# Graph network on one core: zero fills move from the counting loop to the front and to ScalarE, four table words are read at once, two large copies are issued in parts

## The reference

```python
x = x + attention_over_edges(layernorm(x), edge_weight1, src, dst, ...)  # 8 heads, softmax per destination, then an FFN
x = x + moe(layernorm(x), top 2 of 8 experts, D=256)
x = x + gnn(layernorm(x), edge_index, ...)    # two layers: h = (x + segment_sum(x[src], dst) / deg) @ W.T + b
x = x + moe_ln(layernorm(x), top 2 of 8 experts, hidden 1024)
```

## Time and profile before

| | us |
|---|---|
| median of 3 runs | 2374.04 (2373.87 to 2379.93) |
| the profiled execution | 2378.78 |
| its span | 2377.0 |
| TensorE busy over the span | 2022.4 (85%) |
| `front`, start to last VectorE instruction | 0 to 98.1 |
| `adjacency`, first to last TensorE instruction | 100.0 to 395.1 |
| fills, SyncE's 20 issues | 120.5 to 335.0 |
| the three large copies, issued | 335.5 to 339.4 |

### The profile page before, as it was taken

One profiled execution on the slowest core, in us unless ns is written; L12 is line 12 of the kernel. 1 busy time (PEld: TensorE's weight loads), 2 busy tenths in 40 slices (PEclk: granted clock), 3 DMA queues, 4 the chain that ended last, 5 costly groups with the idle time before them and its releaser, 6 DMA issues. The chain is left out here.

```text
span 2377.0 us, 46115 instructions
## 1 busy us (share of the span) xinstructions
PE 2022.4 (85%) x10757; PEld 1611.7 (68%) x10758; DVE 1399.4 (59%) x3191; ACT 1199.6 (50%) x2508; POOL 848.9 (36%) x859
## 2 busy tenths in 40 slices
PE   7777865888888888869996495799999889999995
PEld 4444433666666666548885385799899877888885
DVE  8688876899999999883445435457425364111111
ACT  2488865777777777622323343455455433222221
POOL 3200000777777777511000667350131303031233
PEclk9899998999999999989995698899999989999998
DMA  4234451777777777510000675434334445565664
GB/s 158 82 151 169 167 191 71 204 206 207 206 208 208 206 206 207 158 47 1 3 1 1 228 219 170 120 107 124 100 104 121 154 158 184 196 219 200 218 225 150
DMA packets 154791, 359.75 MB, mean 151 GB/s; under 512 B 23634, under 2 KB 107415, under 8 KB 150615
## 3 DMA queue, kind: packets, MB, share of 16 engines
q1 hardware_dynamic: 98664, 202.78, 25.6%
q0 software_dynamic: 45520, 145.80, 21.7%
q10 hardware_dynamic: 10528, 10.23, 1.3%
HBM read 276.75 MB, written 78.00 MB: 149 GB/s over the span
## 5 line engine op out<-in xcount | busy, mean ns | idle before, releaser
L1024 POOL DMA_INDIRECT kv_pair<-kv,gather_idx x448 | 440.7, 984 | 147.7 <-issue 131.0
L3401 PE MATMUL ge_p<-ge_y_high,ge_counts_wide 128*128 128x256 f32 (+1 forms) x1250 | 325.1, 298 | 3.7 <-ACT ge_counts_wide L2692 1.7
L1133 PE MATMUL p_edge_q<-QX_kept,onehot_turned 128*128 x904 | 263.0, 414 | 72.1 <-ACT onehot_turned L1096 68.4
L3401 PE MATMUL ge_p<-ge_y_low,ge_counts_wide 128*128 128x256 f32 (+1 forms) x1250 | 309.3, 286 | 0.0
L1133 PEld LDWEIGHTS p_edge_q<-QX_kept,onehot_turned 128*128 128x128 f32 x904 | 154.6, 191 | 178.1 <-issue 163.0
L3401 PEld LDWEIGHTS ge_p<-ge_y_high,ge_counts_wide 128*128 128x128 f32 x1250 | 243.1, 194 | 7.8 <-DVE R_kept L2897 2.4
L3401 PEld LDWEIGHTS ge_p<-ge_y_low,ge_counts_wide 128*128 128x128 f32 x1250 | 243.6, 195 | 1.3
L1141 PE MATMUL p_sums<-R_kept 128*128 128x265 f32 x896 | 237.6, 387 | 0.3 <-DVE R_kept L1034 0.3
L901 PE MATMUL adj_p<-adj_onehot_src,adj_onehot_key 128*128 128x416 f16 x1030 | 204.1, 345 | 30.7 <-issue 15.7
L3527 PE MATMUL ge_p<-ge_y,ge_pack 128*128 128x256 f32 x928 | 213.0, 389 | 8.3 <-ACT ge_column_sums L2790 4.6
L2692 ACT CAST ge_counts_wide<-ge_counts 128x1664 fp32r<-128x1664 uint16 (+1 forms) x100 | 152.6, 1527 | 125.5 <-PE ge_p L3401 125.5
(11 more groups left out here) (615 smaller groups left out, 3791.7 us busy)
## 6 DMA issues: line engine op xcount, KB each, us to landing
ge_pack<-experts SPq DMA_DIRECT2D x29, 2052.0 KB, 8.7
ge_counts<-adj SPq DMA_DIRECT2D x400, 104.0 KB, 2.3
adj<-adj_counts SPq DMA_DIRECT2D x100, 208.0 KB, 1.9
slots_in<-R_kept SPq DMA_DIRECT2D x10, 896.0 KB, 3.6
slots_out<-R_kept SPq DMA_DIRECT2D x10, 896.0 KB, 3.6
experts_rows<-slots_in SPq DMA_DIRECT2D x30, 256.0 KB
ge_column_sums<-slots_in SPq DMA_DIRECT2D x30, 256.0 KB, 6.7
slots_out<-experts_y ACTq DMA_DIRECT2D x29, 256.0 KB, 2.6
```

Of the source, the lines that this page charges most:

```text
L1024: pool.indirect_dma_start(kv[r][:, j, :], None, a["kv"], bass.IndirectOffsetOnAxis(ap=idx[r][:, j:j + 1], axis=0)).then_inc(kv_in[r], 16)
L1133: mm = pe.matmul(pQ[q][:, j, 0:QW], oht[q][:, j, :], QX[:, at(w), :].squeeze(1), start=True, stop=True)
L3401: mm = pe.matmul(bank[:, off:off + D], wide[parity][:, j * P:(j + 1) * P], part[:, at(m), :].squeeze(1), start=opening and off == 0 and pa ...
```

## The change

1. **Fills.** The 20 fills of `slots_in` and `slots_out` leave SyncE's loop. ScalarE issues them in `front`, one ahead of each of the tiles 2 to 21, before that tile's copy of the next `hT`. It waits once that `R` is zero, and at the end of the block for all 20 to have landed.
2. **Words.** Each of the three engines reads four packed words with one load at the head of a turn, in place of one word per window. ScalarE is one window ahead, so its group starts at window 1 of the turn; its last, unrolled turn loads three.
3. **Sums and row numbers.** The zeros for `ACC` go in ten parts of two rows of 26 (271 KB each), one behind each of the turns 0 to 9, and one part of six rows behind turn 9. `WHERE` goes the same way behind the turns 10 to 19 (131 KB each) and a last part of six rows.

```diff
+        zeros_set, slots_filled = sem("zeros_set"), sem("slots_filled")
+        FILL_FROM, FILLS = 2, 10
+        slots = [a[name].rearrange("(p r) d -> p r d", p=P) for name in ("slots_in", "slots_out")]
+        PART = slots[0].shape[1] // FILLS
...
-            pool.memset(k["R"][:], 0.0)
+            pool.memset(k["R"][:], 0.0).then_inc(zeros_set, 1)
...
             act.wait_ge(units_set, HR)
+            act.wait_ge(zeros_set, 1)
             for n in range(NT):
                 b = n % 2
+                if 0 <= n - FILL_FROM < 2 * FILLS:
+                    table_, part = divmod(n - FILL_FROM, FILLS)
+                    act.dma_start(slots[table_][:, at(PART * part, PART), :],
+                                  k["R"][:, 0:PART, :]).then_inc(slots_filled, 16)
                 if n + 1 < NT:
                     copy_turned(n + 1)
...
+            act.wait_ge(slots_filled, 16 * 2 * FILLS)
...
-            packed = eng.value_load(k["WTAB"][0:1, at(w)], min_val=0, max_val=128 * VPACK - 1)
+        def words_of(kind, w, count):
+            return nc.values_load_multi_w_load_instructions(k["WTAB"][0:1, at(w, count)], engines=[kind], min_val=0,
+                                                            max_val=128 * VPACK - 1)[1]
...
+        def over_windows(eng, kind, step_of):
+            with eng.Fori(0, TURNS) as i:
+                words = words_of(kind, TURN * i, TURN)
+                for b in range(TURN):
+                    step_of(words[b], TURN * i + b, b, i)
...
-            for s_ in range(2):
-                with sp.Fori(FILLS * s_, FILLS * (s_ + 1)) as i:
-                    for b in range(TURN):
-                        window(TURN * i + b, b, i)
-                    sp.dma_start(slots[s_][:, at(PART * i - PART * FILLS * s_, PART), :],
-                                 k["R"][:, 0:PART, :]).then_inc(zeros_out, 16)
...
-            sp.dma_start(sums[:, over:], zeros).then_inc(zeros_out, 16)
-            sp.dma_start(sums[:, 0:over], zeros[:, 0:over]).then_inc(zeros_out, 16)
-            sp.dma_start(k["WHERE"][:].rearrange("p n c -> p (n c)"), a["places"]).then_inc(zeros_out, 16)
+            with sp.Fori(0, FILLS) as i:
+                for b in range(TURN):
+                    window(TURN * i + b, b, i)
+                zero_sums(at(SPREAD * i, SPREAD), SPREAD)
+            zero_sums(slice(DONE, NT + 1), NT + 1 - DONE)
+            with sp.Fori(FILLS, 2 * FILLS) as i:
+                for b in range(TURN):
+                    window(TURN * i + b, b, i)
+                sp.dma_start(k["WHERE"][:, at(SPREAD * i - DONE, SPREAD), :],
+                             places[:, at(SPREAD * i - DONE, SPREAD), :]).then_inc(zeros_out, 16)
+            sp.dma_start(k["WHERE"][:, DONE:, :], places[:, DONE:, :]).then_inc(zeros_out, 16)
...
-            last_onehot(0, 0, 0)
-            with act.Fori(0, NW // TURN - 1) as i:
+            last_onehot(words_of(ENG.Activation, 0, 1)[0], 0, 0)
+            with act.Fori(0, TURNS - 1) as i:
+                words = words_of(ENG.Activation, TURN * i + 1, TURN)
```

More of the change, by code:

```diff
@@ L764, in adjacency @@
     nc, a, C = k["nc"], k["a"], k["C"]
-    TURN = 4
+    TURN, ENG = 4, mybir.EngineType
     with ExitStack() as s:
@@ L816, in window, with zero_sums @@
                 sp.dma_start(a["adj"][at(w)].rearrange("o q d s -> (o q d) s"), out[b][:]).then_inc(stored[b], 16)
-            for s_ in range(2):
-                with sp.Fori(FILLS * s_, FILLS * (s_ + 1)) as i:
-                    for b in range(TURN):
-                        window(TURN * i + b, b, i)
-                    sp.dma_start(slots[s_][:, at(PART * i - PART * FILLS * s_, PART), :],
-                                 k["R"][:, 0:PART, :]).then_inc(zeros_out, 16)
-            zeros, sums = (t[:].rearrange("p n c -> p (n c)") for t in (k["R"], k["ACC"]))
-            over = sums.shape[1] - zeros.shape[1]
-            sp.dma_start(sums[:, over:], zeros).then_inc(zeros_out, 16)
-            sp.dma_start(sums[:, 0:over], zeros[:, 0:over]).then_inc(zeros_out, 16)
-            sp.dma_start(k["WHERE"][:].rearrange("p n c -> p (n c)"), a["places"]).then_inc(zeros_out, 16)
+            def zero_sums(rows, count):
+                sp.dma_start(k["ACC"][:, rows, :].rearrange("p n c -> p (n c)"),
+                             zeros[:, 0:count * VWC]).then_inc(zeros_out, 16)
+            zeros = k["R"][:].rearrange("p n d -> p (n d)")
+            SPREAD = (NT + 1) // FILLS
+            DONE = SPREAD * FILLS
+            with sp.Fori(0, FILLS) as i:
[9 more added lines that the diff above has]
+            sp.dma_start(k["WHERE"][:, DONE:, :], places[:, DONE:, :]).then_inc(zeros_out, 16)
             with sp.Fori(2 * FILLS, TURNS) as i:
@@ L842, in _, with window @@
             low = C[:, C_IOTA:C_IOTA + P].unsqueeze(1).to_broadcast(wide)
-            def window(w, b, i):
+            def window(word, w, b, i):
                 p = b % 2
-                f, m, v0 = chunks_of(dve, w, TURN // 2 * i + b // 2)
+                f, m, v0 = chunks_of(word, TURN // 2 * i + b // 2)
                 with dve.Fori(0, m) as j:
@@ L858, in window @@
                         ins.then_inc(last_made[p], 1)
-            over_windows(dve, window)
+            over_windows(dve, ENG.DVE, window)
             dve.wait_ge(root_ready, 1)
@@ L882, in _, with window @@
         def _(pe):
-            def window(w, b, i):
+            def window(word, w, b, i):
                 p = b % 2
-                _, m, v0 = chunks_of(pe, w, TURN // 2 * i + b // 2)
+                _, m, v0 = chunks_of(word, TURN // 2 * i + b // 2)
                 def add_nothing(first):
@@ L904, in window @@
                 add_nothing(False).then_inc(summed, 1)
-            over_windows(pe, window)
+            over_windows(pe, ENG.PE, window)
         @block.scalar
```

27 lines of the change are left out of this document (12 added, 15 removed).

## The result

The changed kernel took 2364.23 us (median of 6 runs, 2361.44 to 2365.69); the kernel before, on the same chip, 2376.07 us (6 runs, 2372.23 to 2380.06). The ratio is 0.9948, with an interval of 0.9934 to 0.9962: faster by 0.5%, about 12 us, and half of the 23.7 us forecast. The measured 2364.23 lies 0.2 us above the range given. The profiled execution took 2365.69 us, its span is 2363.9.

A forecast was written before the change was run, and what follows sets the result against it. TensorE bounds front; in adjacency engines wait for each other, with gaps from register loads during fills. Gains 14.7 + 11.0, less 1.0 for parts and 1.0 for front, make 23.7 us: forecast 2350.3 us, range 2342 to 2364.

The forecast's parts named there:

- The bound: In adjacency no engine is full; engines wait for each other through buffer pairs, and register loads slow down during fills.
- Fills and large copies: Counting turns in adjacency: moving fills and splitting large copies gains 14.7 us, 6.2 from fills and 8.5 from copies.
- if every turn takes the 10.36 us of the quiet two: Adjacency: all 24 turns were given the mean of two late turns without fills, 10.63 and 10.08 us, totalling 248.6 us.
- Words: Adjacency: reading four words per load shortens turns from 10.36 to 9.90 us, gaining 11.0 us; other end 19.7.
- if it costs as one, it is in the 9.90: Loop head in adjacency: a four-word load priced like a single load adds nothing beyond the 9.90 us turn.
- the rival of words priced as whole loads: Loop head: each word costs a full load, from no change (2372) to slower (2392); chance 0.04, mild form 0.04.
- the way from 10.36 us down to VectorE's own work: Adjacency turns: removing three of four loads per engine can gain towards VectorE's 9.42 us, plus the changes of window.
- my own term of 0.46 us a turn: Adjacency: gain per turn from bunched words, 10.36 to 9.90 us, with 0.12 us gaps at four windows; 24 turns, 11.0 us.
- Small parts: Zeros and row numbers spread behind 20 adjacency turns cost 1.0 us, between 0 and 1.8 us.
- Front: Twenty fills issued by ScalarE in front cost 1 us, between 0 and 8; DMA share 0.97, issues fit in 1.40 us.
- rival about the DMA engines: In front, DMA at 300 rather than 404 GB/s lands the last fill late, costing 8 us, 2357; chance 0.08.
- the issue: Rival in front: ScalarE held at each issue until its fill lands, 44 us lost against 24.7 gained, 2393; chance 0.02.

The follow-up runs named there:

- e1: Changed kernel with packed words read one by one again, fills in front and small parts kept: 2349.01 us, ratio 0.9910 to the kernel before.
- e3: Kernel before with only the zeros of the sums and the row numbers in small parts; fills stay in the loop: ratio 0.9960.
- e4: Kernel before with only the 20 fills moved to ScalarE in the front; large copies and single words kept: ratio 0.9946.
- e7: Changed kernel with two words per load on all three engines, two loads a turn: median turn 10.38 us, ratio 0.9935 to the kernel before.
- e9: Changed kernel with ScalarE checking its four words' bounds twice, eight more register instructions at the loop's head: median turn 11.54 us, 2383.07 us in one run.
- after: The changed kernel itself, in its first measurement and profile: 2364.23 us, ratio 0.9948 to the kernel before, median turn 10.67 us.
- e8: The changed kernel unchanged, measured again on another chip: ratio 0.9941 to the kernel before, median turn 10.67 us.
- e10: Changed kernel with ScalarE reading its four words by four single loads at the loop's head: median turn 11.25 us, 2380.83 us in one run.
- e5: Changed kernel with four words at once on ScalarE only, one per window on VectorE and TensorE: median turn 11.23 us, ratio 1.0025 to the kernel before.

## Why the prediction was wrong

**The bound.** Right in kind: in `adjacency` the engines wait for each other, and the gaps with no releaser come with loads and grow with fills. e1 and e3 show it directly, 9.2 us of such gaps on ScalarE without fills, 17.7 with them.

**Fills and large copies: the mechanism right, the term too small.** The sum gave 14.7 us less 1.0 for the parts; e1 shows 21.6. The step that failed is "if every turn takes the 10.36 us of the quiet two". The two were 10.63 and 10.08 us, the first of them the turn right behind the stall. Without fills turns take 9.96 us (e4) or 9.97 (e1). So the fills were worth some 0.70 us a turn, not 0.31: over the first 20 turns e4 takes 13.7 us less than before (212.87 and 226.54), where the sum had 6.2. For the large copies the sum had 8.5, and e3, parts included, shows 9.2: 10.0 less over the last four turns, 0.8 more over the first 20.

**Words: the wrong sign.** The sum gave a gain of 11.0 us; it was a loss of 14.8. Two steps failed. The first is "if it costs as one, it is in the 9.90". It doesn't: the head went to 1.82 us, past the 1 us at which the text said the forecast would be wrong, and close to the 1.85 (0.46 a word) of the rival of words priced as whole loads. The eight register instructions behind the load were named, and priced at nothing; they are 0.11 us each. The second is what the three removed loads would bring, "the way from 10.36 us down to VectorE's own work". Without fills they are nearly hidden beside a conversion of 0.83 us: e1 has gaps of 0.37, 0.16 and 0 us, and a turn of 9.97 with all its loads where the sum had 9.90 without three of them. The row of the Square without a gap had shown it. Bunched, four words have one such cover, and single ones had one each. The row was read against a rule that made the loads too dear, and not against my own term of 0.46 us a turn.

The Trainium skill ("DMA: Bandwidth & Descriptors", latency and other measured facts) says that the compiler unrolls loops four times to amortise the floor of a load. Here only 0.53 us a turn was exposed (0.37 + 0.16 + 0 in e1), so there was little to amortise: the form with four words costs 0.70 us a turn more than that with one.

**The rival of words priced as whole loads had nearly the right head and a wrong base.** Its 0.46 us a word fits the head of four, but e7 and e9 show another make-up: register instructions at 0.11 us, and a rest that does not go evenly by the word. With a head of 1.82 us its formula gives 9.34 + 1.82 = 11.16 us a turn; it was 10.67. The 9.34 came from the quiet pair, 20.71 us with 22 instructions on ScalarE. The long stretch of the same rows has 140 in 14 turns, 125.64 / 14 = 8.97 us; after has 8.75, and 8.75 + 1.82 = 10.57 is the measured turn but for 0.1. Twice the short stretch was used as a base where the long one stood beside it.

**Small parts.** Forecast 1.0 us, bounds 0 to 1.8; e1 against e4 shows 2.35 us over seven turns at the same clock, above the upper bound, by one execution of each. **Front.** Forecast 1.0 us, bounds 0 to 8; the first window `b` = 3 starts at 114.46 in after, 113.59 in e8, 114.49 in e1, 113.59 in e4, against 113.95, 114.19 and 113.92 before: up to 0.6 us on either side, so none that can be seen. The share of 0.97, the issue of 0.3 to 0.4 us and its cover by the room ahead of `hT` held. Neither rival about the DMA engines or the issue came true.

**Together.** 21.6 - 14.8 = 6.8 us in the stage, where 14.7 + 11.0 - 1.0 = 24.7 stood. Two errors of opposite sign, +7.9 on fills and -25.8 on words, left the direction right. The measured total is some 5 us better than the stage, and that part is not explained.

The version that follows from this is e1: fills in `front`, small parts, words one by one. It is 0.9% faster than the kernel before, and in the profiled executions it reaches `attention_max` at 377.7 us, the changed kernel at 392.0.

## What to carry to other kernels

Before bunching small loads or register work at a loop's head, look at what runs on the engine while each one is issued: spread out, each hides behind an instruction, and bunched, all but one are exposed (here 1.82 us in one gap against 0.53 in two). Count the register instructions behind a load, bounds among them; they had a price of 0.11 us each on ScalarE, and they stand on every engine that reads the word. Take a turn's length and an engine's busy time per turn from the longest undisturbed stretch, not from two turns next to a stall. And set the sum of the turns beside their median: the median hid here what the parts cost.

## What was not expected of the hardware

- Register instructions on ScalarE at 0.11 us each (e9: 0.90 us for eight), and further loads in a row at some 0.07 us each (e10, by estimate).
- Fills of 896 KB every turn, at a mean DMA share of 0.42, cost 0.70 us of a turn of 10.67, although no engine waited for a fill.
- With fills issued by ScalarE and stores by SyncE, the 16 DMA engines held 370 GB/s at a share of 0.93 over 61 us, and a pipeline with room for 1.4 us per tile did not slow down.
- Taking a gap away from two engines made the turn longer while the third kept its own (e5 11.23 us, after 10.67). It is not TensorE's clock: e5's turns of 11.2 us ran at a granted clock of 1.00, as those of after did.
- The same code took from 597.6 to 604.6 us for the stretch from `attention_max` to its end, in three executions.
